# Sandwich block on one core: the three PE transposes of each tile's pipeline replaced by DVE block transposes and DRAM scratches, in 15 stages

## What is computed

```python
x = x + _layernorm(attn(_layernorm(x)))
x = x + _layernorm(ffn(_layernorm(x)))
```

```python
q = hidden_states @ w_q.T
...
sq = elu_plus_one(q)
sk = elu_plus_one(k)
...
A = jnp.einsum('bid,bjd->bij', sqi, ski) * mask
num = jnp.einsum('bij,bje->bie', A, vi) + jnp.einsum('bid,bde->bie', sqi, S_kv)
den = A.sum(-1) + jnp.einsum('bid,bd->bi', sqi, z)
out = num / jnp.clip(den, EPS, None)[..., None]
S_kv = S_kv + jnp.einsum('bcd,bce->bde', ski, vi)
```

```python
w = jax.nn.silu(jnp.einsum('btd,bthkd->bthk', hidden_states, de) * jax.nn.softmax(scores, axis=-1))
experts_states = jnp.einsum('bthk,bthkd->btd', w, ue)
dense = jnp.einsum('bti,di->btd', jax.nn.silu(jnp.einsum('btd,id->bti', hidden_states, W_up)), W_down)
return dense + experts_states
```

## Time and profile before

| | |
|---|---|
| median of 3 runs | 3030.0 us |
| profiled execution, its own time | 3034.47 us |
| its span | 3032.7 us |
| PE busy | 2970.0 us |
| ACT busy | 2532.4 us |
| DVE busy | 2420.2 us |
| POOL busy | 1955.8 us |
| mean granted clock | 0.992 |

### The profile page before, as it was taken

The page is one execution under the profiler, slowest core; times in us unless marked ns, Lnnn a source line. Parts: engine busy times, 40 slices in busy tenths (PEclk is TensorE's granted clock), DMA queues, the critical chain, the costliest instruction groups (busy, mean ns, idle before and its releaser), DMA issues.

```text
span 3032.7 us, 46880 instructions
## 1 busy us (share of the span) xinstructions
PE 2970.0 (98%) x15402; PEld 2431.6 (80%) x15402; DVE 2420.2 (80%) x5764; ACT 2532.4 (84%) x3854; POOL 1955.8 (64%) x2455
## 2 busy tenths in 40 slices
PE   6899999999999999999999999999999999999996
PEld 5678888888887888888888888888878888888875
DVE  3878888888887888888888788888878888888884
ACT  3888888888888888888888888888888888888884
POOL 2666666666666666666666666666666666666763
PEclk8999999999999999999999999999999999999998
...
GB/s 96 96 130 128 122 126 129 125 125 127 129 124 129 127 126 124 127 126 124 131 129 124 122 131 123 129 126 128 124 129 127 125 124 128 125 124 130 129 124 120
DMA packets 188360, 378.33 MB, mean 125 GB/s; under 512 B 18899, under 2 KB 122324, under 8 KB 188116
## 3 DMA queue, kind: packets, MB, share of 16 engines
...
q1 hardware_dynamic: 134868, 173.99, 18.3%
...
...
## 4 chain that ended last, share of the span: by engine, by line
PE 95%; DMA 2%; issue 1%; DVE 1%; POOL 1%; ACT 1%; SPq 0%; POOLq 0%; DVEq 0%
PE banks L529 86%; PE banks L547 3%; PE banks L534 2%; PE banks L608 2%; PE banks L601 1%; DMA wexp<-wexp 1%; DMA sums<-in_L_ffn_keys_dram 0%; SPq L353 0%; POOL sums L418 0%; DMA gT<-w_way 0%; DVE w_blocks L783 0%; PE banks L513 0%; POOL rstd L404 0%; PE banks L520 0%; PE banks L498 0%
## 5 line engine op out<-in xcount | busy, mean ns | idle before, releaser
L418 POOL TENSOR_TENSOR sums<-scores 128x1024 f32<-128x1024 f32 x512 | 1033.9, 2019 | 749.7 <-ACT scores L653 749.7
L404 POOL TENSOR_TENSOR rstd<-var_eps,minus_half 128x1 f32<-128x1 f32 x512 | 498.0, 1110 | 69.0 <-DVE var_eps L855 35.7
L529 PE MATMUL banks<-ue,gT 128*128 128x256 f32 x2048 | 528.9, 412 | 13.7 <-DMA gT<-w_way 13.7
L529 PEld LDWEIGHTS banks<-ue,gT 128*128 128x128 f32 x2048 | 502.7, 336 | 16.1 <-DMA gT<-w_way 14.5
L529 PE MATMUL banks<-xn2T,wupT 128*128 128x128 f32 x4096 | 498.8, 275 | 3.1 <-DVE state L821 3.1
L529 PEld LDWEIGHTS banks<-xn2T,wupT 128*128 128x128 f32 x4096 | 487.4, 192 | 10.1 <-DVE state L821 3.6
L529 PE MATMUL banks<-deT,xn2T 128*128 128x512 f32 x1024 | 481.3, 592 | 0.0
L529 PE MATMUL banks<-wdownT,hT 128*128 128x256 f32 x2048 | 465.0, 380 | 6.0 <-ACT y_sb L650 6.0
L529 PEld LDWEIGHTS banks<-wdownT,hT 128*128 128x128 f32 x2048 | 380.5, 191 | 54.2 <-issue 7.5
L529 PEld LDWEIGHTS banks<-deT,xn2T 128*128 128x128 f32 x1024 | 185.1, 190 | 130.8 <-issue 123.4
L783 DVE STREAM_TRANSPOSE w_blocks<-wexp 128x1024 f32<-128x1024 f32 x128 | 260.9, 2039 | 4.8 <-DMA wexp<-wexp 4.6
(11 more groups left out here) (135 smaller groups left out, 6695.9 us busy)
## 6 DMA issues: line engine op xcount, KB each, us to landing
wexp<-wexp POOLq DMA_DIRECT2D x128, 1024.0 KB, 8.0
wexp<-wexp POOLq DMA_DIRECT2D x128, 512.0 KB, 4.6
w_way<-w_blocks SPq DMA_DIRECT2D x128, 512.0 KB, 2.6
gT<-w_way SPq DMA_DIRECT2D x512, 128.0 KB, 3.0
x_in<-_attn_hidden_states_dram SPq DMA_DIRECT2D x128, 128.0 KB, 2.9
out_dram<-x_out SPq DMA_DIRECT2D x128, 128.0 KB, 1.7
...
```

Of the source, the lines that this page charges most:

```text
L404: return nc.gpsimd.tensor_tensor(rstd[:, n, m:m + 1], var_eps[:, n, m:m + 1], minus_half[:, :], ALU.pow)
L418: return nc.gpsimd.tensor_tensor(sums[:, k, :, :], scores[:, k, 0:XIN].unsqueeze(2).broadcast_to([P, XIN, NKEYS]), scores[:, HEADS + k, :] ...
L529: last = nc.tensor.matmul(out, lhs(c), rhs(c), start=(start and c == 0), stop=(stop and c == chunks - 1))
```

## The change

Three operands are no longer transposed by PE: xn1, xn2 and sigma(k). For each, DVE transposes 32x32 blocks (128x256) into a tile (xn1_blocks, xn2_blocks, sk_blocks), SP writes that to a DRAM scratch (xn1_way, xn2_way, sk_way) and gathers it in four transfers into xn1T, xn2T or sk_nat, in which the two chunks are the innermost index: PE reads a chunk of them with a step of two elements (8 bytes). ACT's three copies out of PSUM are gone. The expert weights are gathered into g_parts, with w_blocks written in order of its columns, and ACT copies g_parts to gT, in which each chunk is contiguous. The pipeline has 15 stages instead of 10, the bodies are ordered anew (in PE's, both halves of up stand together ahead of q and k), buffers are deeper (x_mid 10, hT 3, v_one 2), and the set-up is cut: the first tile's x, keys and W_rq are loaded earlier, and the transposes of down_embed and W_down are done inside the first tile's step (late).

```diff
-    MID_SLOTS = 8
+    MID_SLOTS = 10
...
-        xn1T = sb("xn1T", [P, DC, P])
-        xn2T = sb("xn2T", [P, 2, DC, P])
+        xn1T = sb("xn1T", [P, 2, P, DC])
+        xn2T = sb("xn2T", [P, 2, P, DC])
         rqk = sb("rqk", [P, 2 * DC, P])
         sig = sb("sig", [P, 2, 2 * DC, P])
-        v_one = sb("v_one", [P, DX])
-        sk_nat = sb("sk_nat", [P, D])
+        v_one = sb("v_one", [P, 2, DX])
+        sk_nat = sb("sk_nat", [P, 2, P, DC])
         at = sb("at", [P, P])
...
+        sk_blocks = sb("sk_blocks", [P, D])
+        sk_way = nc.dram_tensor("sk_way", [2, P, D], fp32).ap()
+        xn1_blocks = sb("xn1_blocks", [P, D])
+        xn1_way = nc.dram_tensor("xn1_way", [2, P, D], fp32).ap()
+        xn2_blocks = sb("xn2_blocks", [P, D])
+        xn2_way = nc.dram_tensor("xn2_way", [2, P, D], fp32).ap()
...
-        hT = sb("hT", [P, 2, IC, P])
-        gT = sb("gT", [P, 2, P, EC])
+        hT = sb("hT", [P, 3, IC, P])
+        gT = sb("gT", [P, 2, EC, P])
+        g_parts = sb("g_parts", [P, BLOCKS, EC, BLOCK])
...
-        STAGES = 10
+        STAGES = 15
...
+            for dst, src in ((wo_in, w_o), (mem_in, memory), (wq_in, w_q), (wk_in, w_k), (wv_in, w_v)):
+                sp.dma_start(dst[:, :, :], src.rearrange("(c p) n -> p c n", p=P)).then_inc(s_w_att, 16)
+            sp.dma_start(x_in[:, 0, :], x_tiles[:, chunk_of(0), seq_of(0), :]).then_inc(s_x_loaded, 16)
+            sp.dma_start(wup_in[:, :, :], W_up.rearrange("(c p) n -> p c n", p=P)).then_inc(s_w_up, 16)
+            sp.dma_start(keys_in[:, :, :, :], keys.rearrange("h k s n -> k h s n")).then_inc(s_w_route, 16)
+            sp.dma_start(wrq_in[:, :, :], W_rq.rearrange("(g n) d -> n g d", n=KDIM)).then_inc(s_w_route, 16)
+            for dst, src, s_in in ((ue, up_embed, s_w_ue), (de_in, down_embed, s_w_de), (wdown_in, W_down, s_w)):
+                sp.dma_start(dst[:, :, :], src.rearrange("(c p) n -> p c n", p=P)).then_inc(s_in, 16)
...
-                    sp.dma_start(dst[j * BLOCK:(j + 1) * BLOCK, :, :].rearrange("p (i t) c -> p i (t c)", t=BLOCK),
+                    sp.dma_start(dst[j * BLOCK:(j + 1) * BLOCK, :, :],
                                  way.rearrange("(i q) (j n) -> j q i n", q=BLOCK, j=BLOCKS)[j]).then_inc(s_in, 16)
 
             def body(t, steady):
+                if t[8] is not None:
+                    sp.wait_ge(s_xn2_blocks_turned, t[8] + 1)
+                    sp.dma_start(xn2_way[t[8] % 2, :, :], xn2_blocks[:, :]).then_inc(s_xn2_blocks_out[t[8] % 2], 16)
+                if t[5] is not None:
+                    sp.wait_ge(s_xn1_blocks_turned, t[5] + 1)
+                    sp.dma_start(xn1_way[t[5] % 2, :, :], xn1_blocks[:, :]).then_inc(s_xn1_blocks_out[t[5] % 2], 16)
+                if t[11] is not None:
+                    sp.wait_ge(s_expert_weights_blocks_turned, t[11] + 1)
+                    sp.dma_start(w_way[t[11] % 2, :, :], w_blocks[:, :]).then_inc(s_expert_weights_blocks_out[t[11] % 2], 16)
+                if t[7] is not None:
+                    wait(sp, s_sk_blocks_turned, t[7] + 1, KEPT)
+                    if t[7] < KEPT:
+                        sp.dma_start(sk_way[t[7] % 2, :, :], sk_blocks[:, :]).then_inc(s_sk_blocks_out[t[7] % 2], 16)
+                if t[11] is not None:
+                    wait(sp, s_expert_weights_T_ready, t[11])
+                    moved(sp, s_expert_weights_blocks_out, t[11], 1)
+                    gather(g_parts[:, :, :, :].rearrange("p i c t -> p i (c t)"), w_way[t[11] % 2, :, :], s_expert_weights_blocks_in[t[11] % 2])
+                if t[8] is not None:
+                    moved(sp, s_xn2_blocks_out, t[8], 1)
+                    gather(xn2T[:, t[8] % 2, :, :].rearrange('p (i t) c -> p i (t c)', t=BLOCK), xn2_way[t[8] % 2, :, :], s_xn2_blocks_in[t[8] % 2])
+                if t[5] is not None:
+                    moved(sp, s_xn1_blocks_out, t[5], 1)
+                    if not steady:
+                        wait(sp, s_v_in_psum, t[5] - 1)
+                    gather(xn1T[:, t[5] % 2, :, :].rearrange('p (i t) c -> p i (t c)', t=BLOCK), xn1_way[t[5] % 2, :, :], s_xn1_blocks_in[t[5] % 2])
                 if t[0] is not None:
                     wait(sp, s_x_loaded, 16 * t[0])
-                    sp.dma_start(x_in[:, t[0] % SLOTS, :], x_tiles[:, chunk_of(t[0]), seq_of(t[0]), :]).then_inc(s_x_loaded, 16)
-                if t[9] is not None:
-                    sp.wait_ge(s_x_out_ready, t[9] + 1)
-                    sp.dma_start(out_tiles[:, chunk_of(t[9]), seq_of(t[9]), :], x_out[:, :]).then_inc(s_x_stored, 16)
-                if t[7] is not None:
-                    sp.wait_ge(s_expert_weights_blocks_turned, t[7] + 1)
-                    sp.dma_start(w_way[t[7] % 2, :, :], w_blocks[:, :]).then_inc(s_expert_weights_blocks_out[t[7] % 2], 16)
-                    moved(sp, s_expert_weights_blocks_out, t[7], 1)
-                    gather(gT[:, t[7] % 2, :, :], w_way[t[7] % 2, :, :], s_expert_weights_blocks_in[t[7] % 2])
+                    if t[0] > 0:
+                        sp.dma_start(x_in[:, t[0] % SLOTS, :], x_tiles[:, chunk_of(t[0]), seq_of(t[0]), :]).then_inc(s_x_loaded, 16)
+                if t[7] is not None:
+                    wait(sp, s_state_add_in_psum, t[7], KEPT)
+                    moved(sp, s_sk_blocks_out, t[7], 1, KEPT)
+                    if t[7] < KEPT:
+                        gather(sk_nat[:, t[7] % 2, :, :].rearrange('p (i t) c -> p i (t c)', t=BLOCK), sk_way[t[7] % 2, :, :], s_sk_blocks_in[t[7] % 2])
+                if t[13] is not None:
+                    sp.wait_ge(s_x_out_ready, t[13] + 1)
+                    sp.dma_start(out_tiles[:, chunk_of(t[13]), seq_of(t[13]), :], x_out[:, :]).then_inc(s_x_stored, 16)
 
...
```

PE, ACT and DVE:

```diff
-                if t[3] is not None:
-                    pe.wait_ge(s_xn1_ready, t[3] + 1)
-                    turn(t_ps, xn1).then_inc(s_xn1T_in_psum, 1)
...
-                                       lambda c: xn2T[:, t[5] % 2, c, :])
+                                       lambda c: xn2T[:, t[10] % 2, :, c])
...
+                if t[7] is not None:
+                    moved(pe, s_xn1_blocks_in, t[7], BLOCKS)
...
-                    moved(pe, s_expert_weights_blocks_in, t[7], BLOCKS)
-                    product(y_ps, EC, lambda c: gT[:, t[7] % 2, :, c], lambda c: ue[:, c, :], start=False).then_inc(s_y_in_psum, 1)
-                if t[4] is not None:
-                    pe.wait_ge(s_xn2_ready, t[4] + 1)
-                    turn(t_ps, xn2).then_inc(s_xn2T_in_psum, 1)
...
+                    product(v_ps, DC, lambda c: xn1T[:, t[7] % 2, :, c], lambda c: wvo[:, c, :]).then_inc(s_v_in_psum, 1)
+                if t[13] is not None:
+                    pe.wait_ge(s_expert_weights_T_ready, t[13] + 1)
+                    product(y_ps, EC, lambda c: gT[:, t[13] % 2, c, :], lambda c: ue[:, c, :], start=False).then_inc(s_y_in_psum, 1)
+                if t[9] is not None:
+                    if t[9] == 0:
+                        pe.wait_ge(s_set_sb, SET_ALL)
+                    moved(pe, s_xn2_blocks_in, t[9], BLOCKS)
+                    product(sc_ps[:, :], DC, lambda c: xn2T[:, t[9] % 2, :, c], lambda c: route[:, c, :]).then_inc(s_route_scores_in_psum, 1)
+                if t[7] is not None:
+                    if t[7] == 0:
+                        late(range(len(parts)))
+                    pe.wait_ge(s_sigma_ready, t[7] + 1)
+                    product(at_ps, DC, lambda c: sig[:, t[7] % 2, DC + c, :], lambda c: sig[:, t[7] % 2, c, :]).then_inc(s_scores_in_psum, 1)
...
-                            last = nc.tensor.transpose(sk_ps[:, c * P:(c + 1) * P], sig[:, t[3] % 2, DC + c, :], ident[:, :])
-                        last.then_inc(s_sk_in_psum, 1)
...
+                            last = nc.tensor.matmul(ds_ps[:, c, :], sk_nat[:, t[8] % 2, :, c], v_one[:, t[8] % 2, :], start=True, stop=True)
...
+                    moved(act, s_expert_weights_blocks_in, t[12], BLOCKS)
+                    nc.scalar.copy(gT[:, t[12] % 2, :, :].rearrange("p c (i t) -> p i c t", t=BLOCK), g_parts[:, :, :, :]).then_inc(s_expert_weights_T_ready, 1)
...
-                    act.wait_ge(s_xn2T_in_psum, t[5] + 1)
-                    nc.scalar.copy(flat(xn2T[:, t[5] % 2, :, :]), t_ps).then_inc(s_xn2T_ready, 1)
...
-                        nc.scalar.copy(sk_nat[:, :], sk_ps).then_inc(s_sk_ready, 1)
...
-                    act.wait_ge(s_xn1T_in_psum, t[3] + 1)
-                    nc.scalar.copy(flat(xn1T), t_ps).then_inc(s_xn1T_ready, 1)
...
+                    dve.wait_ge(s_xn1_ready, t[5] + 1)
+                    moved(dve, s_xn1_blocks_out, t[5] - 1, 1)
+                    nc.vector.transpose(turned_blocks(xn1_blocks, DC), blocks(xn1[:, :])).then_inc(s_xn1_blocks_turned, 1)
+                if t[8] is not None:
+                    dve.wait_ge(s_x_mid_rstd, t[8] + 1)
+                    normed(xn2[:, :], x_mid[:, t[8] % MID_SLOTS, :], LN_M, t[8] % 2).then_inc(s_xn2_ready, 1)
```

(11 more changed lines are left out.)

576 lines of the change are left out of this document (287 added, 289 removed).

## The result

The changed kernel takes 2904.3 us (median of 4 runs, 2901.0 to 2905.1) against 3029.4 before (4 runs, 3028.5 to 3034.3): a ratio of 0.958, with a 95% interval of 0.9565 to 0.9599. That is 125 us less, where 161 were forecast (2869). The time lies within the range, 35 us above the forecast.

The account below looks back on a forecast made before the run. PE, busy throughout mid-span, was taken as the bound: its step falls from 23.01 by 1.24 to 21.77 us. Start 141, middle 2627 and end 103 sum to a 2871 us span, hence 2869 us; range 2838 to 3000.

Parts of the forecast that it names:

- -0.66: On PE, three pairs of transposes a step (xn1, xn2, sigma(k)) go, 0.22 us each: 0.66 us a step saved.
- -0.49: PE's product with gT reads its stationary operand contiguously: 3.45 us instead of 3.94, 0.49 us a step saved.
- The stand at q: PE's short wait before the q product, put down to ScalarE's eviction of up: 0.09 us a step goes.
- The lower end: DVE's four transposes run at the rate of plain DVE work: 2.2 us together, and PE never stands.
- PE's reads with the 8-byte step: Up, q and k stream operands with an 8-byte step: taken as nothing, bounds nothing to +6.5 us a step.
- B: Rival: the 8-byte step costs PE half a rate, +0.6 us a step, 2946 us; 8 in 100.
- C: Rival: the 8-byte step costs PE's moving operand what 32 bytes cost the weight load, 3701 us; 5 in 100.
- The place that decides: Loop from sigma through DVE's transposes to the causal mask: 7.5 us plus transposes, against PE's 9.95 us.
- The middle part: From the first product with gT to that of tile 121: 121 x 21.77 - 7.0 = 2627 us.
- The start: Time until gT of tile 0: 122.4 - 5 for earlier set-up + 24 for two added steps = 141 us.
- The DMAs and SP: Turned operands come over DRAM, landing 3.0 us after issue; SP issues 22 DMAs a step, not 7: costed at nothing.
- D: Rival: DMA contention makes the sum over the heads late for the w transpose, 3034 us if landing takes 9; 6 in 100.

Follow-up runs that it names:

- both_off: Kernel before, without its transposes of xn1, xn2 and sigma(k) on PE and with gT read contiguously: 2888.7 us, one run.
- w_turn_32b: Changed kernel, with VectorE's large transpose of the expert weights writing with its old 32-byte step again: 2975.3 us, one run.
- moving_contig: Changed kernel, with the up, q and k products reading the same bytes contiguously instead of with an 8-byte step: 2897.7 us.
- steps: Changed kernel, with up's halves reading a constant tile at 32-byte and 16-byte steps, q contiguous, k at 8 bytes: 3361.4 us, one run.
- mask_early: Changed kernel, with VectorE's statistics of x and a short add moved from ahead of the causal mask to behind it: 2895.1 us.
- setup_first: Changed kernel, with the late part of the set-up ahead of the pipeline again, not in the first steps: 2903.7 us, one run.
- early_contig: Changed kernel, with VectorE's statistics behind the causal mask and xn1T and xn2T laid out contiguously, interleaved by the DRAM write: 2963.9 us.

## Why the forecast was right, and where it was 35 us off

**What PE loses: right.** -0.66 and -0.49 came out as such, alone and together. The stand at q is gone too: q takes 0.91 after the change and 0.90 contiguously, against 0.98 in the kernel before (1522.05 to 1523.03) and in both_off, which keeps its order (1515.54 to 1516.52). That it was the wait for ScalarE's eviction no run shows.

**VectorE's transposes: right.** The lower end held: 2.24 us for the four, 2.2 taken. The reason given for it, the 32-byte write, is shown by w_turn_32b. The estimate of 2.4 ns a column, which the prediction set against itself, doesn't fit this shape: 1.16 us for 1024 columns are 1.1 ns.

**PE's reads with the 8-byte step: the term that was mis-sized.** I took nothing, between nothing and +6.5. It is 0.07 in up (3.63 against twice 1.78) and 0.03 in q and k (1.81 against 1.78): 0.10 a step, 12 us in the middle part. Of this, moving_contig, which changes nothing else, shows 0.08. The trace sides neither with my argument, that half of a line used costs nothing, nor with B and C. The Trainium skill (Advanced Engine Details and Errata, SBUF Cachelines) puts the penalty at accesses that each go to another line of 16 bytes; steps agrees where it bites (0.227 and 0.233 us at 16 and 32 bytes). At 8 bytes, where the rule leaves full speed, PE's moving operand takes 2% more, while VectorE's transpose takes no more (0.36 us, both ways).

**The place that decides: right in kind, and too tight to be free.** PE's way from k's end to the masked product is 9.95 us as computed (1507.49 to 1517.44). VectorE's way was 7.5 + 2.2 = 9.7 in the forecast, and 9.64 in one step of the trace, 9.80 in the next (1529.36 to 1539.16). What I left out is that sigma can start late, behind the selection that waits for POOL; then nothing is left, and the step grows by 0.06, in four steps by 0.3 to 0.6. That the loop binds is shown by mask_early; that the late sigma is why is read from the rows, and no run takes it out by itself. Over the 113 full steps of the middle their mean is 21.92, 0.05 above the 21.87 of PE's rows: 5 us.

**The middle part** is 20.7 us longer: these 12 and 5 us, and 3 more from my correction for steps that lack a product with state. I took 7.0 off. In the changed kernel only the last six steps of this stretch are short, by 3.8 us together. That the same correction closed for the kernel before was luck: its short steps were the last seven of the stretch, 1.09 us each, and what they lack is the update of the state and the transposes of sigma(k) (0.87 and 0.22), not the product with the state.

**The start** is 8.2 us later. It begins 2.1 us earlier than before and not 5, because the first xn1T lands at 37.8 (9.8 us of waiting for it). From the first product to the first with gT are 111.4 us against 82.5, 28.9 more for two added steps, where I took 24. But the late part of the set-up is in it: in setup_first, which has it ahead, the same stretch is 105.7 us, so the added steps cost 11.6 us each, near the 12 I took, and 5.7 us are the late part, which I put at nothing. The two longest waits there:

```profile
PE banks L639 <- DVE at L872: 8.6, 5, 4.1
PE banks L579 <- DVE sig L817: 6.5, 4, 3.2
```

These are PE's waits from 25 to 150 us, the one of 9.8 us aside: in all, number, longest. These sizes hold for one profile each; among the versions with the same set-up the first product with gT varies by 3 us (149.2 to 152.4).

**The DMAs and SP: right in this kernel, for a narrower reason than given.** Mid-span no product waits for a transfer in the changed kernel. But the reason given, that each operand is used most of a step or more after it could land, holds for xn1T (19 us in hand) and not for xn2T, which takes 6.3 us to land, not 3.0, and has 4.6 in hand. The page's part 3 and 6, against the earlier trace rows:

```profile
q1 hardware_dynamic: 405588, 272.68, 31.9%
...
wexp<-wexp POOLq DMA_DIRECT2D x128, 512.0 KB, 4.6
...
g_parts<-w_way SPq DMA_DIRECT2D x512, 128.0 KB, 3.0
...
xn2T<-xn_way SPq DMA_DIRECT2D x512, 32.0 KB, 6.3
```

Three times the packets take 1.7 times the share, and the heads' sum lands in 4.6 us as before. So D, which feared the contention, was wrong about the place (and its sum was wrong: with 6.5 us of lead, landing in 9 gives 2869 + 127 x 2.5 = 3187, not 3034). But I priced the 15 issues that SP gets at nothing without adding up its queue. They were free because of its pauses, and early_contig shows what six more, with smaller packets, cost: 69 us.
